# First cross-attention scores placed among the last transposes of the first norm, the last query projection in halves behind them

## Chip, cores and metric

The kernel runs on one core of one Trainium2 chip. The metric is the device time of one execution in microseconds (us); lower is better.

## The reference

A decoder layer with the norm behind each part, on x of 2 x 1024 tokens with 256 features (2048 tokens in all), in float32:

```
x = layernorm(x + causal_self_attention(x))          # 16 heads of 16
x = layernorm(x + cross_attention(x, ctx, mask))     # 64 context rows per batch, biases, 16 heads
x = layernorm(x + mixture_of_experts(x))             # 16 experts, 4 per token, one shared expert
```

What the change touches is the seam between the first two lines. Of the cross-attention:

```
q = split_heads(queries @ Wq + bq)
scores = einsum('bhqd,bhkd->bhqk', q, k) / sqrt(16)
scores = where(mask, -1e15, scores)
attn = softmax(scores); ctx = einsum('bhqk,bhkd->bhqd', attn, v)
```

## The kernel before

The work goes over 16 tiles of 128 tokens (NT = 16; tiles 0 to 7 are the first batch, TB = 8). Every engine has its own program, written out by hand, and takes it strictly in order; semaphores are the only link. The result of a matmul goes to one of eight banks of `ps`.

**First norm.** TensorE (the loop over `t` in `range(NT + 4)`, L1634) writes the output projection of tile t to bank t % 2 (L1641). VectorE adds it to x and takes the statistics (`norm_stats`, L1061 to L1067), GpSimd the reciprocal root (`power`, L758), VectorE applies both (`norm_apply`, L1072) and counts `ln_done`. TensorE, three tiles behind, transposes the normed tile (`transpose_x`, L1631) and ScalarE copies it to `xT` (L863, `xT_kept`). In the same loop ScalarE rounds expert weights (`w_high`, L856), GpSimd subtracts (`w_low`, L765), and VectorE keeps the keys and values of the context (`keep_kv`, L1046 and L1054; `kv_kept` is 20 at the end).

**Query projection.** Behind every fourth transposed tile TensorE projects the queries of these four tiles, 512 columns, in two halves of 128 features, o = 0 and 1, to banks 6 and 7 (L1657, four matmul records each; `xq_ready`). ScalarE copies each half with its bias to `q2` (L870, `xq_kept`). Halves 7 and 8 are those of tiles 12 to 15.

**Cross-attention.** It follows one list, `XO`, that each engine reads. Step n works on half o = n % 2 of the heads of tile n // 2. The kinds that matter here, with their lags in steps: "S" (lag 0), scores on TensorE to bank n % 2: two records of q times keys (L1729) and one of the mask (L1731); VectorE takes the maximum (L1310) and subtracts it (L1314, `xs_sub`), ScalarE the exponential (L889, `xp_exp`), and at odd n with n // 2 below 4 a pair of expert weights (L856). "T" (lag 2): TensorE transposes the exponentials (L1738), ScalarE copies them (L896, `xpT_kept`). "V" (lag 4): times the values (L1748). "P", "Y" (lags 5 and 6, at odd steps): transpose (L1758) and output projection (L1765), and with "Y" the second norm begins, its root on GpSimd (L758). "X", "L": transpose of the normed tile and the router's logits (L1783). GpSimd waits for `xq_ready` to be 8, clears `biased` (L772) and then at each "S" below 16 adds a bias to a tile of x (L777), with a pair of `w_low` at each odd one.

TensorE enters the list behind these waits: `ln_in` NT, `xT_kept` NT, `kv_kept` 20, `xq_kept` 8, `mask_ready` 1. `xq_kept` 8 means that the last half of the last projection is copied. Scores 0 and 1 need queries of tile 0 alone.

Behind the cross-attention come the routing, the scatter of the rows (L788), the shared expert, 79 blocks of expert work and the last norm.

Of the kernel before, what the change touches and what calls it, by code (L numbers as in the profile page):

```python
# [28 lines left out]
ACT = mybir.ActivationFunctionType  # L29
AX = mybir.AxisListType  # L30

P = 128
B, S, D, H, DH = 2, 1024, 256, 16, 16
KC = D // P
T = B * S
NT = T // P
TB = S // P
S2 = 64
# [24 lines left out]
CH = 512  # L63
# [127 lines left out]
def build(nc, a, out, qk_parts, l_dram, slots, sums_of, marks):  # L191
    with ExitStack() as ctx:
# [18 lines left out]
        xT = sb("x_T", [P, KC, T], F32)  # L211
# [17 lines left out]
        kbd = vg_flat[:, 0:2048].rearrange("p (o b h k) -> p o b h k", o=2, b=B, h=8)  # L229
# [15 lines left out]
        q2 = on_mem[:, 0:4096].rearrange("p (o t) -> p o t", o=2)  # L245
# [25 lines left out]
        mask = wqkv_mem[:, 3 * D:3 * D + NT * S2 // 2].bitcast(BF16).rearrange("p (t k) -> p t k", t=NT)  # L271
        w_mem = sb("w_o1_xqkv", [P, 2048], F32)
        wo1 = w_mem[:, 0:512].rearrange("p (c n) -> p c n", c=GB // 2)
        wxq, wxk, wxv = (w_mem[:, 512 * i:512 * i + 512].rearrange("p (c n) -> p c n", c=KC) for i in (1, 2, 3))
        used = [0]

        def over_w(words):
# [14 lines left out]
        bq = sb("b_q", [P, 2], F32)  # L292
# [3 lines left out]
        identb = sb("ident_b", [P, P], BF16)  # L296
# [61 lines left out]
               for u, at in enumerate((0, 512, 2048))]  # L358
        hsp = nc.alloc_sbuf_tensor_at("block_h", [P, 3, 2, P], F32R, offset=on_at + 4 * (4096 + 3072))
        ps = ctx.enter_context(nc.psum_tensor("ps", [P, 8, CH], F32))  # L360
# [22 lines left out]
        y_ready, ln_in, ln_chain, ln_pow, ln_done, xT_ready, xT_kept = (  # L383
            sem(n) for n in ("y_ready", "ln_in", "ln_chain", "ln_pow", "ln_done", "xT_ready", "xT_kept"))
        kv_ready, kv_kept, mask_ready, xq_ready, xq_kept = (
            sem(n) for n in ("kv_ready", "kv_kept", "mask_ready", "xq_ready", "xq_kept"))
        xs_ready, xs_max, xs_sub, xp_exp, xpT_ready, xpT_kept, xo_recip, xo_norm, xoT_ready = (
            sem(n) for n in ("xs_ready", "xs_max", "xs_sub", "xp_exp", "xpT_ready", "xpT_kept", "xo_recip", "xo_norm",
                             "xoT_ready"))
# [410 lines left out]
        def _(act):  # L800
            for n in range(NQK):
# [11 lines left out]
                if n >= 4:  # L813
                    t, more = n % 2, 1 + (n - 4) // 2
# [34 lines left out]
            act.wait_ge(ld_late, 16 * 16)  # L849
            act.wait_ge(b_ready, NB * NG)  # L850

            def w_high(e):

                act.wait_ge(ld_we[e // 4], 32)
                for raw, high in zip(raw_of(e), part_of(e, 0)):
                    nc.scalar.activation(high, raw, ACT.Copy).then_inc(w_hi, 1)  # L856

            for t in range(NT + 1):
                if W_TILE <= t < NT:
                    w_high(t - W_TILE)  # L860
                if t < NT:
                    act.wait_ge(xT_ready, t + 1)
                    nc.scalar.activation(xT[:, :, P * t:P * t + P],  # L863
                                         ps[:, 2 + t % 2, 0:D].rearrange("p (c s) -> p c s", c=KC),
                                         ACT.Copy).then_inc(xT_kept, 1)
                if t and t % 4 == 0:
                    for o in range(2):
                        n = (t // 4 - 1) * 2 + o
                        act.wait_ge(xq_ready, n + 1)
                        nc.scalar.activation(q2[:, o, CH * (t // 4 - 1):CH * (t // 4)], ps[:, 6 + o, :],  # L870
                                             ACT.Identity, bias=bq[:, o:o + 1]).then_inc(xq_kept, 1)
            def shared(c):
                act.wait_ge(g_ready, c + 1)
                wait(act, h_done, c - 1)
# [7 lines left out]
                                         ps[:, c % 2 + 2 * u, :], ACT.Copy).then_inc(y_moved, 1)  # L882

            for kind, n in XO:
                if kind == "S":
                    act.wait_ge(xs_sub, n + 1)
                    if n >= 2:
                        act.wait_ge(xpT_ready, n - 1)
                    nc.scalar.activation(px[:, n % 2, :], sx[:, n % 2, :], ACT.Exp, scale=SCALE).then_inc(xp_exp, 1)  # L889
                    if n % 2 and W_ACT + n // 2 < E:  # L890
                        w_high(W_ACT + n // 2)
                if kind == "T":
                    act.wait_ge(xpT_ready, n + 1)
                    if n >= 2:
                        act.wait_ge(xo_ready, n - 1)
                    nc.scalar.activation(pTx[:, n % 2].rearrange("p r s -> p (r s)"), ps[:, 2 + n % 2, :],  # L896
                                         ACT.Copy).then_inc(xpT_kept, 1)
                if kind == "O":
                    act.wait_ge(xoT_ready, n + 1)
                    if n >= 2:  # L900
                        act.wait_ge(y_ready, NT + n - 1)
                    nc.scalar.activation(oTx[:, n % 2].rearrange("p o s -> p (o s)"), ps[:, 5, 0:D],
                                         ACT.Copy).then_inc(xo_kept, 1)
                if kind == "Z":
                    act.wait_ge(ln_shift, n + 1)
                    nc.scalar.activation(x[:, n, :], x[:, n, :], ACT.Identity, bias=nmr[:, n % 4:n % 4 + 1],
                                         scale=rstd[:, n % 4:n % 4 + 1]).then_inc(ln_done, 1)
                if kind == "X":
                    act.wait_ge(xT_ready, NT + n + 1)
                    nc.scalar.activation(xT[:, :, P * n:P * n + P],  # L910
                                         ps[:, 7, 0:D].rearrange("p (c s) -> p c s", c=KC),
                                         ACT.Copy).then_inc(xT_kept, 1)
                if kind == "L":
                    act.wait_ge(r_logit, n + 1)
                    size = GROUPS[n]
                    nc.scalar.activation(score[:, FIRST[n]:FIRST[n + 1], :],
                                         ps[:, 7, D:D + size * E].rearrange("p (t e) -> p t e", t=size),
                                         ACT.Exp, scale=-1.0).then_inc(r_kept, 1)
                if kind == "E":
                    shared(n)  # L920
                if kind == "A" and n >= 2:
                    move_y(n)
# [578 lines left out]
        def _(pe):  # L1501
# [67 lines left out]
            for kind, n in P1:  # L1569
                if kind in ("qk0", "qk1"):  # L1570
                    b, o, t = QK[n]
# [57 lines left out]
            def transpose_x(t, bank):  # L1629
                for k in range(KC):  # L1630
                    last = nc.tensor.transpose(ps[:, bank, P * k:P * k + P], x[:, t, P * k:P * k + P], identf[:])  # L1631
                last.then_inc(xT_ready, 1)

            for t in range(NT + 4):  # L1634
                if t < NT:
                    if t >= 2:
                        pe.wait_ge(ln_in, t - 1)
                    pe.wait_ge(o_done, (t // TB + 1) * GB // 2)
                    for q in range(GB // 2):
                        pair = on[:, t // TB * GB + 2 * q + 1, P * (t % TB):P * (t % TB) + P]  # L1640
                        last = nc.tensor.matmul(ps[:, t % 2, 0:D], pair, wo1[:, q, :], start=(q == 0),  # L1641
                                                stop=(q == GB // 2 - 1))
                    last.then_inc(y_ready, 1)
                s = t - 3
                if 0 <= s < NT:
                    pe.wait_ge(ln_done, s + 1)
                    if s >= 2:
                        pe.wait_ge(xT_kept, s - 1)
                    transpose_x(s, 2 + s % 2)
                s -= 1  # L1650
                if s >= 0 and s % 4 == 3:
                    pe.wait_ge(xT_kept, s + 1)
                    for o in range(2):
                        if s >= 4:
                            pe.wait_ge(xq_kept, s // 4 * 2 + o - 1)
                        for k in range(KC):
                            last = nc.tensor.matmul(ps[:, 6 + o, :], wxq[:, k, P * o:P * o + P],  # L1657
                                                    xT[:, k, P * (s - 3):P * (s + 1)], start=(k == 0), stop=(k == KC - 1))
                        last.then_inc(xq_ready, 1)

            def project(c, part):

# [52 lines left out]
                last.then_inc(r_rank, 1)  # L1715


            pe.wait_ge(ln_in, NT)
            pe.wait_ge(xT_kept, NT)
            pe.wait_ge(kv_kept, 20)  # L1720
            pe.wait_ge(xq_kept, 8)
            pe.wait_ge(mask_ready, 1)
            tiles, logits = 0, 0
            for kind, n in XO:
                if kind == "S":
                    t, o = n // 2, n % 2
                    if n >= 2:
                        pe.wait_ge(xs_sub, n - 1)
                    nc.tensor.matmul(ps[:, n % 2, :], q2[:, o, P * t:P * t + P],  # L1729
                                     kbd[:, o, t // TB].rearrange("p h k -> p (h k)"), start=True, stop=False)  # L1730
                    nc.tensor.matmul(ps[:, n % 2, :], identb[:], mask[:, t, :].unsqueeze(1).to_broadcast([P, 8, S2]),  # L1731
                                     start=False, stop=True).then_inc(xs_ready, 1)
                if kind == "T":
                    pe.wait_ge(xp_exp, n + 1)
                    if n >= 2:
# [5 lines left out]
                if kind == "V":  # L1741
                    t, o = n // 2, n % 2
# [218 lines left out]
```

## Time and profile before

| | |
|---|---|
| median of 3 runs | 642.4 us (641.43 to 643.92) |
| profiled execution, its own time | 642.46 us |
| its span, first to last instruction | 640.7 us |
| mean granted TensorE clock | 0.977 |
| busy: TensorE, VectorE, ScalarE, GpSimd | 91%, 74%, 57%, 48% |
| first scores of the cross-attention start at | 340.9 us |

The span is from the first to the last instruction; the time of an execution is a little longer. A granted clock of 1.00 is the full one (2.4 GHz), 0.50 the lower one (1.2 GHz).

### The profile page before, as it was taken

To read this page: it belongs to the slowest core of one execution; us is meant where nothing else is said; L and a number is where in the kernel's file an instruction comes from. 1 tells how busy PE (TensorE), PEld (TensorE's weight loads), DVE (VectorE), ACT (ScalarE), POOL (GpSimd) and SP (SyncE) were. 2 spreads that over 40 slices of the span, in tenths; PEclk is the share of its full clock that TensorE was granted. 3 is DMA by queue.
4 is the path that set the end of the run, shared out by engine and by line. 5 is a ranking of instruction groups with operands and counts; after the bars stand their busy time and mean duration, and the time that the engine had idled before them with its cause. 6 is when DMAs were issued, how large, how long until landed. Compare 5 with 4: busy or idle time off the path is not lost.

```text
span 640.7 us, 12791 instructions
## 1 busy us (share of the span) xinstructions
PE 583.5 (91%) x3766; PEld 356.6 (56%) x3766; DVE 475.0 (74%) x1306; ACT 364.1 (57%) x742; POOL 310.2 (48%) x395
## 2 busy tenths in 40 slices
PE   6978899999999999898879999999877999998994
PEld 2634434433343443225444777778546899998861
DVE  2388788887888889305965787776555987998896
ACT  2335366766666676782464644535315677776645
POOL 5414314142533433255587550647564777775650
PEclk9999899999999999999999998979987999999999
DMA  5967797172543710002930000212234896669957
GB/s 183 204 179 160 137 276 104 26 104 56 71 86 53 109 25 3 20 20 71 381 127 0 1 2 1 79 64 85 86 107 135 247 293 224 213 190 305 318 181 249
DMA packets 47773, 82.92 MB, mean 129 GB/s; under 512 B 12023, under 2 KB 28919, under 8 KB 45815
## 3 DMA queue, kind: packets, MB, share of 16 engines
q1 hardware_dynamic: 40844, 62.68, 39.0%
q0 software_dynamic: 6864, 19.44, 8.2%
q8 instruction: 33, 0.54, 0.4%
q14 instruction: 32, 0.25, 0.1%
HBM read 53.81 MB, written 32.48 MB: 135 GB/s over the span
## 4 chain that ended last, share of the span: by engine, by line
PE 53%; DVE 23%; DMA 8%; issue 5%; SPq 4%; ACT 4%; POOL 3%; POOLq 0%; DVEq 0%; ACTq 0%
DVE neg_max L986 9%; PE ps L1540 8%; PE ps L1564 8%; PE ps L1831 6%; PE ps L1521 4%; PE ps L1729 3%; PE ps L1854 3%; PE ps L1748 3%; DMA v_group<-expert_slots 3%; DMA stacks<-m_rows 2%; PE ps L1810 2%; POOL expert_slots L788 2%; PE ps L1765 2%; PE ps L1578 2%; ACT temps L831 2%
## 5 line engine op out<-in xcount | busy, mean ns | idle before, releaser
L986 DVE TENSOR_REDUCE neg_max<-ps 128x1 f32<-128x512 f32 (+3 forms) x304 | 181.5, 654 | 29.9 <-PE ps L1526 15.9
L831 ACT ACTIVATE temps<-ps 128x1024 f32<-128x1024 f32 (+1 forms) x192 | 146.4, 812 | 72.3 <-PE ps L1540 72.0
L724 POOL TENSOR_SCALAR_AFFINE_SELECT temps<-temps 128x256 f32<-128x256 f32 x128 | 52.3, 412 | 141.7 <-ACT temps L831 140.3
L1540 PE MATMUL ps<-stacks 99*128 99x512 bf16 (+3 forms) x384 | 94.3, 331 | 4.5 <-DMA stacks<-m_rows 2.9
L795 POOL DMA_INDIRECT expert_outputs<-x_T,w_o_xqkv x79 | 78.1, 988 | 32.8 <-issue 16.8
L1521 PE MATMUL ps<-stacks 96*128 96x512 bf16 (+3 forms) x320 | 86.9, 320 | 7.1 <-DVE neg_max L986 6.8
L1564 PE MATMUL ps<-temps,v_group 128*32 128x512 f32 (+3 forms) x768 | 81.8, 498 | 1.7 <-POOL temps L724 0.6
L788 POOL DMA_INDIRECT expert_slots<-x_tok,w_o_xqkv x64 | 62.5, 976 | 26.5 <-issue 17.2
L1831 PE MATMUL ps<-w_split,block_x 128*128 x474 | 71.9, 289 | 0.7 <-DVE block_x L1398 0.7
L1540 PEld LDWEIGHTS ps<-stacks 99*128 99x128 bf16 x384 | 27.2, 98 | 75.2 <-ACT temps L831 55.5
L1831 PEld LDWEIGHTS ps<-w_split,block_x 128*128 128x128 f32 x474 | 63.8, 195 | 1.1 <-issue 1.1
L1521 PEld LDWEIGHTS ps<-stacks 96*128 96x128 bf16 x320 | 30.9, 98 | 38.3 <-DVE neg_max L986 21.1
L1854 PE MATMUL ps<-w_split,block_h 128*128 x237 | 48.6, 314 | 0.3 <-ACT x_T L951 0.3
L758 POOL TENSOR_TENSOR ln_rstd<-ln_var_eps,minus_half 128x1 f32<-128x1 f32 x32 | 18.8, 589 | 60.4 <-DVE ln_var_eps L1067 60.3
L889 ACT ACTIVATE o_norm<-o_norm 128x512 f32<-128x512 f32 x32 | 20.1, 629 | 48.5 <-DVE o_norm L1314 48.4
L1526 PE MATMUL ps<-stacks 128*128 128x128 bf16 x256 | 44.4, 221 | 2.9 <-DVE neg_max L986 1.6
L938 ACT ACTIVATE o_norm<-ps 128x128 f32<-128x128 f32 x79 | 21.9, 278 | 31.2 <-PE ps L1831 30.2
L1578 PE MATMUL ps<-x_T,w_qkv 128*128 128x512 f32 x64 | 31.9, 639 | 6.0 <-DMA x_T<-in_xT 6.0
L1398 DVE TENSOR_TENSOR block_x<-ps,block_x 128x256 fp32r<-128x256 f32 x79 | 33.1, 420 | 5.5 <-ACT block_x L930 4.3
L1729 PE MATMUL ps<-v_group,o_norm 128*128 128x512 f32 x64 | 34.8, 627 | 1.4 <-ACT o_norm L870 1.0
L1310 DVE TENSOR_REDUCE x_max<-ps 128x8 f32<-128x512 f32 x32 | 22.1, 690 | 18.3 <-PE ps L1731 17.8
L704 POOL TENSOR_TENSOR temps<-temps 128x1024 bf16<-128x1024 f32 (+1 forms) x10 | 17.4, 1741 | 36.9 <-ACT temps L812 36.9
(221 smaller groups left out, 1085.2 us busy)
## 6 DMA issues: line engine op xcount, KB each, us to landing
stacks<-qk_parts SPq DMA_DIRECT2D x96, 128.0 KB
v_group<-expert_slots SPq DMA_DIRECT2D x79, 138.5 KB
qk_parts<-temps SPq DMA_DIRECT2D x6, 768.0 KB, 4.6
w_raw<-in_w SPq DMA_DIRECT2D x4, 1024.0 KB, 10.1
early_parts<-expert_outputs SPq DMA_DIRECT2D x4, 1024.0 KB, 8.1
expert_slots<-in_pad SPq DMA_DIRECT2D x16, 138.5 KB
expert_slots<-in_pad SPq DMA_DIRECT2D x1, 2077.5 KB
x_T<-in_xT SPq DMA_DIRECT2D x4, 512.0 KB, 6.3
```

Source lines behind the costliest of these rows:

```text
L724: nc.gpsimd.affine_select(diag, diag, [[0, 2], [1, P]], ALU.is_ge, zero, base=0, channel_multiplier=-1).then_inc(b_cut, 1)
L788: pool.indirect_dma_start(slots, bass.IndirectOffsetOnAxis(ridx[:, t, k:k + 1].bitcast(U32), 0), xe[:, t, :], None).then_inc(scattered[q], 16)
L795: pool.indirect_dma_start(sums_of, bass.IndirectOffsetOnAxis(idxs[:, b:b + 1].bitcast(U32), 0), yb[:, b % YB, :], None).then_inc(landed[b ...
L831: nc.scalar.activation(pt[:, n % 4, :, 0:w], ps[:, 2 + 2 * (n % 2):4 + 2 * (n % 2), 0:w], ACT.Exp, scale=SCALE).then_inc(b_exp, 1)
L986: nc.vector.tensor_reduce(nmx[:, c, h0:h0 + nh, i], ps[:, A_BANKS[n % 3], 0:w * nh].rearrange("p (h k) -> p h k", h=nh), axis=AX.X, op=ALU ...
L1521: last = nc.tensor.matmul(ps[:, A_BANKS[n % 3], w * s:w * s + plain], qs[0:KR, ua, h0 + s, P * i:P * i + P], ks[0:KR, ua, h0 + s, CH * c:C ...
L1540: last = nc.tensor.matmul(ps[:, bank, 0:w], ks[0:KM, u, 2 * pr + s, P * j:P * j + P], qs[0:KM, u, 2 * pr + s, q0:q0 + w], start=True, stop ...
L1564: last = nc.tensor.matmul(ps[HS * h:HS * h + HS, 6, CH - w:CH], vg[:, u, j, h, :], pt[:, (2 * p + h // 2) % 4, h % 2, 0:w], start=(j == 0) ...
L1578: last = nc.tensor.matmul(ps[:, 2 + 2 * (n % 2) + q, :], wqkv[:, t, k, P * o:P * o + P], xT[:, k, S * b + CH * q:S * b + CH * q + CH], sta ...
L1729: nc.tensor.matmul(ps[:, n % 2, :], q2[:, o, P * t:P * t + P], kbd[:, o, t // TB].rearrange("p h k -> p (h k)"), start=True, stop=False)
L1831: last = nc.tensor.matmul(ps[:, 2 + b % 2, 0:D], xsp[b % 3][:, xp, k, :], w13s[:, bass.ds(expert[b], 1), wp, at:at + 2 * INTER], start=(k ...
L1854: last = nc.tensor.matmul(ps[:, 6 + b % 2, 0:D], hsp[:, b % 3, hp, :], w2s[:, bass.ds(expert[b], 1), wp, :], start=(n == 0), stop=(n == 2))
```

## The change

Scores 0 and 1 leave the head of the list on TensorE and stand in the loop of the first norm, ahead of the wait for the norm of tile 15 and its transposes. They wait for `kv_kept` 20, `mask_ready` 1, `xq_kept` 6 (three of the four query projections) and `ln_in` 15 and 16 (their banks). The last query projection leaves the loop: its half o = 0 stands ahead of scores 2, its half o = 1 ahead of scores 3, and ScalarE's two copies of the halves stand ahead of exponentials 2 and 3. The list is entered behind `xT_kept` NT alone; `xq_kept` 8 is waited for ahead of scores 24 (tile 12), the first that need it. VectorE's and GpSimd's programs are as before.

```diff
@@ ScalarE
+            def keep_queries(c, o):
+
+                act.wait_ge(xq_ready, 2 * c + o + 1)
+                nc.scalar.activation(q2[:, o, CH * c:CH * c + CH], ps[:, 6 + o, :],
+                                     ACT.Identity, bias=bq[:, o:o + 1]).then_inc(xq_kept, 1)
...
-                if t and t % 4 == 0:
+                if t and t % 4 == 0 and t < NT:
                     for o in range(2):
-                        n = (t // 4 - 1) * 2 + o
-                        act.wait_ge(xq_ready, n + 1)
-                        nc.scalar.activation(q2[:, o, CH * (t // 4 - 1):CH * (t // 4)], ps[:, 6 + o, :],
-                                             ACT.Identity, bias=bq[:, o:o + 1]).then_inc(xq_kept, 1)
+                        keep_queries(t // 4 - 1, o)
...
             for kind, n in XO:
+                if kind == "S" and n in (2, 3):
+                    keep_queries(NT // 4 - 1, n - 2)
@@ TensorE
+            def query_projection(c, o):
+
+                pe.wait_ge(xT_kept, 4 * c + 4)
+                if c:
+                    pe.wait_ge(xq_kept, 2 * c + o - 1)
+                for k in range(KC):
+                    last = nc.tensor.matmul(ps[:, 6 + o, :], wxq[:, k, P * o:P * o + P],
+                                            xT[:, k, CH * c:CH * c + CH], start=(k == 0), stop=(k == KC - 1))
+                last.then_inc(xq_ready, 1)
+
+            def cross_scores(n):
+
+                t, o = n // 2, n % 2
+                nc.tensor.matmul(ps[:, n % 2, :], q2[:, o, P * t:P * t + P],
+                                 kbd[:, o, t // TB].rearrange("p h k -> p (h k)"), start=True, stop=False)
+                nc.tensor.matmul(ps[:, n % 2, :], identb[:], mask[:, t, :].unsqueeze(1).to_broadcast([P, 8, S2]),
+                                 start=False, stop=True).then_inc(xs_ready, 1)
+
+            def early_scores():
+
+                pe.wait_ge(kv_kept, 20)
+                pe.wait_ge(mask_ready, 1)
+                pe.wait_ge(xq_kept, 6)
+                for n in range(2):
+                    pe.wait_ge(ln_in, NT - 1 + n)
+                    cross_scores(n)
...
                 s = t - 3
                 if 0 <= s < NT:
+                    if s == NT - 1:
+                        early_scores()
                     pe.wait_ge(ln_done, s + 1)
...
                 s -= 1
-                if s >= 0 and s % 4 == 3:
-                    pe.wait_ge(xT_kept, s + 1)
+                if 0 <= s < NT - 1 and s % 4 == 3:
                     for o in range(2):
-                        if s >= 4:
-                            pe.wait_ge(xq_kept, s // 4 * 2 + o - 1)
...
+                        query_projection(s // 4, o)
...
-            pe.wait_ge(ln_in, NT)
             pe.wait_ge(xT_kept, NT)
-            pe.wait_ge(kv_kept, 20)
-            pe.wait_ge(xq_kept, 8)
-            pe.wait_ge(mask_ready, 1)
...
+                if kind == "S" and n in (2, 3):
+                    query_projection(NT // 4 - 1, n - 2)
+                if kind == "S" and n >= 2:
+                    if n == NT + TB:
+                        pe.wait_ge(xq_kept, 8)
+                    pe.wait_ge(xs_sub, n - 1)
+                    cross_scores(n)
```

## Rows read from the trace of the kernel before

**Rows 1.** The page: TensorE's busy time, and the granted clock by fortieths of the span.
```profile
PE 583.5 (91%) x3766; PEld 356.6 (56%) x3766; DVE 475.0 (74%) x1306; ACT 364.1 (57%) x742; POOL 310.2 (48%) x395
...
PEclk9999899999999999999999998979987999999999
```

**Rows 2.** Chain that ended last, 330 to 352: start us, us, what.
```profile
330.53 0.69 ACT o_norm L870
...
334.56 5.41 PE ps L1657 x8
...
339.99 0.70 ACT o_norm L870
...
340.93 1.10 PE ps L1729 x2
...
342.28 0.70 DVE x_max L1310
...
343.75 1.12 PE ps L1729 x2
344.88 0.22 PE ps L1731
345.09 0.44 PE ps L1738 x4
...
347.04 0.86 PE ps L1729 x2
```

**Rows 3.** Timeline of TensorE: start us, us, instructions, [idle before, its releaser].
```profile
324.14 0.44 PE L1631 MATMUL ps<-ident_f,x_tok 128*128 128x128 f32 x2 [0.39 <-DVE x_tok L1072]
...
326.89 3.60 PE L1657 MATMUL ps<-x_T,w_o_xqkv 128*128 128x512 f32 x8
...
333.36 0.44 PE L1631 MATMUL ps<-ident_f,x_tok 128*128 128x128 f32 x2 [2.03 <-DVE x_tok L1072]
...
342.94 0.38 PE L1731 MATMUL ps<-w_qkv,ident_b 128*128 128x512 bf16 x1
```

**Rows 4.** Timeline of VectorE.
```profile
331.96 1.35 DVE L1072 TENSOR_SCALAR x_tok<-x_tok,ln_mean_var,ln_rstd 128x256 f32<-128x256 f32 x1 [1.13 <-POOL ln_rstd L758]
342.28 0.69 DVE L1310 TENSOR_REDUCE x_max<-ps 128x8 f32<-128x512 f32 x1 [8.97 <-PE ps L1731]
343.01 0.69 DVE L1314 TENSOR_TENSOR o_norm<-ps,x_max 128x512 f32<-128x512 f32 x1
```

**Rows 5.** Timeline of GpSimd.
```profile
340.02 0.37 POOL L772 MEMSET w_o_xqkv<- 128x320 f32 x1 [6.13 <-PE ps L1657]
...
351.21 1.97 POOL L765 TENSOR_TENSOR w_split<-w_raw,w_split 128x512 fp32r<-128x512 f32 x2
359.11 0.55 POOL L758 TENSOR_TENSOR ln_rstd<-ln_var_eps,minus_half 128x1 f32<-128x1 f32 x1 [5.94 <-DVE ln_var_eps L1067]
```

**Rows 6.** Windows: stretch, us, busy by engine (instructions), granted clock, DMA share, GB/s.
```profile
386.00:390.00 4.00, 4.00 (x17) 2.83 (x16) 2.35 (x5) 0.85 (x3) 0.00 (x0) 0.57 0.00 0
...
442.00:446.00 4.00, 4.00 (x38) 3.90 (x37) 1.54 (x5) 2.03 (x5) 3.06 (x5) 1.00 0.28 106
```

**Rows 7.** Windows around the last query projection; busy: TensorE, weight loads, VectorE, ScalarE, GpSimd.
```profile
331.40:334.50 3.10, 0.44 (x2) 0.20 (x2) 1.35 (x1) 3.10 (x9) 2.49 (x4) 1.00 0.00 0
335.30:338.80 3.50, 3.50 (x5) 1.35 (x4) 0.00 (x0) 0.69 (x1) 0.00 (x0) 0.51 0.00 0
```

**Rows 8.** Timeline of ScalarE.
```profile
324.61 0.38 ACT L863 ACTIVATE x_T<-ps 128x256 f32<-128x256 f32 x1 [0.31 <-PE ps L1631]
...
328.81 0.69 ACT L870 ACTIVATE o_norm<-ps,b_q 128x512 f32<-128x512 f32 x1 [1.34 <-PE ps L1657]
...
334.12 0.38 ACT L863 ACTIVATE x_T<-ps 128x256 f32<-128x256 f32 x1
...
343.73 0.63 ACT L889 ACTIVATE o_norm<-o_norm 128x512 f32<-128x512 f32 x1 [3.05 <-DVE o_norm L1314]
...
345.59 0.92 ACT L856 ACTIVATE w_split<-w_raw 128x512 fp32r<-128x512 f32 x2
```

More of the change, by code:

```diff
@@ L1650, in _ @@
                 s -= 1
-                if s >= 0 and s % 4 == 3:
-                    pe.wait_ge(xT_kept, s + 1)
+                if 0 <= s < NT - 1 and s % 4 == 3:
                     for o in range(2):
-                        if s >= 4:
-                            pe.wait_ge(xq_kept, s // 4 * 2 + o - 1)
[L1656 to L1659, printed above, removed]
+                        query_projection(s // 4, o)
             def project(c, part):
@@ L1715, in ranks @@
                 last.then_inc(r_rank, 1)
-            pe.wait_ge(ln_in, NT)
             pe.wait_ge(xT_kept, NT)
-            pe.wait_ge(kv_kept, 20)
-            pe.wait_ge(xq_kept, 8)
-            pe.wait_ge(mask_ready, 1)
             tiles, logits = 0, 0
             for kind, n in XO:
[L1725 to L1732, printed above, removed]
+                if kind == "S" and n in (2, 3):
[5 more added lines that the diff above has]
+                    cross_scores(n)
                 if kind == "T":
```

## The prediction

> **What bounds the kernel now.** I read the page first: TensorE is busy 91% of the span [rows 1]. That share is a mean over stages, so I went to the place of the change, between 326 and 352 us. The view to read there is the chain of waits, which names at every moment the work that the end hung on [rows 2]. The reader sees one thread with no alternative: ScalarE keeps the sixth half of the queries (330.53) and goes on with expert weights and tile copies; then come eight matmuls of the last query projection (334.56, 5.41 us), ScalarE's copy of its second half (0.70), the first scores on TensorE, VectorE's maximum (0.70) and subtraction (0.70), and from 343.75 on TensorE without a gap: scores, transposes, scores. The engines one by one say who was idle meanwhile. TensorE waited 2.03 us ahead of the transposes of tile 15, for VectorE [rows 3]. VectorE ended the norm of tile 15 at 333.31 and had nothing until 342.28, 8.97 us [rows 4]. GpSimd had nothing for 6.13 us up to 340.02, when the last half of the projection was done [rows 5]. So up to 343.75 the stage is a relay with latency in it, and behind that it is bound by TensorE; the windows further on show TensorE busy 4.00 of 4.00 us [rows 6], so what the relay loses, the end loses, and what it saves, the end gets, if the later stages are only shifted.
>
> Last I looked at the granted clock. It is 1.00 while TensorE has 0.44 us of work in the 3.10 us from 331.4, and 0.51 in the 3.50 us from 335.3, though the engine is then busy all the time [rows 7]: it ran at 1.2 instead of 2.4 GHz behind the gap. Eight matmuls of the same shape took 3.60 us at 326.89 [rows 3].
>
> **The change, part by part.** Nothing is removed from the work: the eight records of the last projection, its two query copies and the six records of scores 0 and 1 have other places.
>
> *Scores 0 and 1 ahead of the transposes of tile 15.* They wait for the sixth query copy, which ends at 330.53 + 0.69 = 331.22 [rows 2]; for the banks of the output projections of tiles 14 and 15, for the keys and for the mask, all of which VectorE has done before its norm at 331.96 and the 1.13 us of idle time ahead of it [rows 4], as it takes its queue in order. From the end of a query copy to the first score goes 0.24 us (339.99 + 0.70 to 340.93) [rows 2], so scores 0 begin at 331.46. Today the pair runs from 340.93 until the next instruction could start 0.22 us into the second mask matmul, at 342.94 + 0.22 = 343.16 [rows 2, 3]: 2.23 us. The pair ends so at 333.69, in the gap of 2.03 us. The transposes that stand behind it start at 333.69 instead of 333.36: 0.33 us late. What is late next is ScalarE's copy of tile 15. It starts 0.47 us behind its transposes where ScalarE is free (324.14 to 324.61) [rows 3, 8], so at 334.16; today it starts at 334.12, since ScalarE was with weights until then (busy 3.10 of the 3.10 us from 331.4) [rows 7, 8]. The edit therefore costs 0.04 us of the 0.33, and the projection starts at 334.60. Without that cover of ScalarE it would cost all 0.33.
>
> *VectorE.* Scores 0 are ready 1.35 us behind their start (340.93 to 342.28), at 332.81, so VectorE goes straight on at 333.33: maximum, subtraction, maximum, subtraction, at 0.70 each (342.28 to 343.01 is 0.73 from start to start) [rows 2, 4]; it ends the second subtraction at 336.2. ScalarE starts its exponential 0.72 us behind the start of a subtraction (343.01 to 343.73) [rows 2, 8]: 334.8 and 336.2. All of this now lies beside the projection.
>
> *The halves of the last projection.* Four matmuls are 3.60 / 2 = 1.8 us, or 1.73 in the chain's counting, where eight stand with 3.45 once the pipe is filled. TensorE's queue is then: half 0 (334.60 to 336.33), scores 2 (0.86 + 0.22 = 1.08, to 337.41), transposes 0 (0.44, to 337.85), half 1 (1.73, to 339.58), scores 3 (to 340.66), transposes 1 (to 341.10), scores 4. One start behind a wait costs 0.26 us more (1.12 + 0.22 at 343.75 against 1.08) [rows 2], so scores 4 start at 341.36, against 347.04 now. Each wait in it is met. Exponential 0 is there at 335.4 for transposes 0. Scores 4 want subtraction 2, which ends near 339.3. Transposes 2 want exponential 2 (near 339.9; ahead of it is the first query copy, which is ready at 334.60 + 1.92 = 336.5, the 1.92 being from the start of a half to its copy, 326.89 to 328.81 [rows 3, 8], but stands behind expert 12's weights of 0.92 us until 337.6). The tightest is ScalarE's second probability copy: in its queue stand between 336.7 and 344.5 two weight pairs (0.92 each), two query copies (0.69), exponentials 2 and 3 (0.63) and copies 0 and 1 [rows 8], and exponential 3 waits for VectorE until 342.5; it ends near 344.5, and TensorE wants it for transposes 3 near 344.7. That is a margin of 0.2 us, and I put 0.2 us in the sum for it. If the cover is gone, each us by which ScalarE is late is a us lost.
>
> *What else is queued behind the moved steps.* On ScalarE the query copies stand ahead of exponentials 2 and 3. On GpSimd the memset waits for the eighth half: 337.85 + 1.92 + about 0.2 = 340.0, and today it starts at 340.02; so GpSimd keeps its old times while the others come forward. Its queue of eight additions of the bias and four weight pairs runs to 351.21 + 1.97 = 353.18, and the first reciprocal root of the second norm is wanted at 359.11 [rows 5], which comes forward to 353.4. Slack 5.94 us before, 0.2 after, and VectorE takes the root only behind another maximum and subtraction. From there a pair of tiles costs GpSimd less than TensorE, and the slack grows again. I cost it at nothing. The edits move no DMA and pass no wait of SP; SP's next wait in this stage is for the last scores. The wait for the eighth copy, now ahead of scores 24, is met some 15 steps earlier.
>
> **The sum.** 347.04 - 341.36 = 5.68 us earlier. It splits in two: the projection took 5.41 where 3.45 would do (1.96 us, the clock), and 3.7 us are the last query copy, the first scores' latency and VectorE's pair, now beside other work. With the 0.2 of margin, 5.5. From the profiled execution, 642.46 us (span 640.7, and 1.8 around it): 642.46 - 5.5 = **637.0 us**. The median of the runs shown is 642.40, so the same sum holds against it.
>
> *Bounds.* What the trace can't show is the clock in the new order. At worst the two halves run as now: 1.96 us are not won, gain 3.5. If they ran wholly at the lower clock the eight would take 6.9 us and the gain would be 5.5 - 3.45 = 2.1. At best ScalarE's margin holds and the gain is 5.7. I take the full clock, since the gap of 3.10 us with 0.44 us of work gets 2.23 us of scores, and the gaps left are of about 0.5 us, of which the run at the full clock ahead has such ones too (0.39 us at 324.14) [rows 3]. Further on there are stretches at the lower clock while TensorE is busy without a gap: in the 4 us from 386 the granted clock is 0.57, which costs 4.00 x (1.00 - 0.57) = 1.7 us; from 442, in a stretch with the same steps of the third group of tiles, it is 1.00 [rows 6]. So such a stretch can come or stay away when the work is shifted, plus or minus 1.7 us for each.
>
> The Trainium skill, TensorE: Matmul & The Clock Gate, section Part 1: The HAM clock gate, says that the monitor runs on its own time, not the kernel's, so that the same kernel changes clock at other places from run to run. By it the 1.96 us need not be in every run of the kernel before, and the median would win between 3.5 and 5.5 us. The trace neither agrees nor disagrees, being of one execution; that the stretches at 386 and 442 differ speaks for it [rows 6].
>
> **The rivals.**
> (a) *The clock part is not won*, because the clock still falls in the new order, or because most runs of before don't have the fall there. For it: 386 and 442 differ [rows 6]. Against it: the profiled execution stands at the median. Gain 3.5: **638.9 us**. The Trainium skill, TensorE: Matmul & The Clock Gate, section Part 1: The HAM clock gate, would let one expect this one.
> (b) *ScalarE becomes the bound in the first eight steps.* For it: a margin of 0.2 us by my own count. Against it: it was idle in the relay (3.05 us ahead of the first exponential alone) [rows 8], and what it gains there it can spend. If its two weight pairs and two query copies are paid in full (2 x 0.92 + 2 x 0.69 = 3.2), the gain is 5.7 - 3.2 = 2.5: **640.0 us**, within 0.5%.
> (c) *The scores are not early*: some wait ahead of them (the sixth copy, the keys) holds them and with them tile 15. Then only the order of the halves changes; one half (1.73) leaves the path to scores 0 but is paid behind it: gain 0, **642.5 us**. Against it: the sixth copy ends at 331.22, and VectorE was through with all that the scores want at 331.96 - 1.13 = 330.83 [rows 2, 4].
> (d) *Slower*: behind the new start the lower clock lasts longer in the part that TensorE bounds (now 343.75 to 386, at 1.00). A us at half the clock loses half a us, so it decides from 2 x 5.5 = 11.0 us of it on; 18 us of it lose 9.0: **646.0 us**. Nothing in the profile speaks for it but that the fall at 386 came while the engine was busy; against it, no fortieth of the span (16 us) has a clock below seven tenths, so none holds more than 0.6 x 16 = 9.6 us at the lower one [rows 1].
>
> **How the numbers follow.** The forecast 0.60, (a) 0.22, (b) 0.10, (c) 0.05, (d) 0.03. The forecast's own range is 635.3 to 638.7, one stretch of 1.7 us either way. The range for 8 in 10 must take in (a): 635.0 to 640.0; (b), (c) and (d) are left out. A change of 0.5% is 3.2 us, about what a measurement of this kernel can tell from none. Faster by more than that, below 639.2: the forecast and most of (a), 0.79. Within: the rest of (a), (b), (c), 0.18. Slower: 0.03.
>
> **What the changed profile would show.** Scores 0 and 1 start at 331.5, and the transposes of tile 15 near 333.7; VectorE's gap of 8.97 us is gone; the projection shows as two groups of four at near 334.6 and 337.9 with 592 ns a matmul and a granted clock of 1.00; scores 4 start near 341.4; GpSimd's memset stays at 340.0 and the first root shows no wait for it. I am wrong if the halves run at a clock of 0.5, if TensorE is idle for ScalarE between 341 and 346, if the first root starts more than 0.6 us behind its input, or if the later stages come forward by less than 5 us.

## The result and the profile after

The changed kernel took 636.28 us in the median of four runs (632.51 to 642.1), the kernel before 643.07 us (641.43 to 643.92). The ratio is 0.9881, with a 95% interval of 0.9833 to 0.993: faster by 7.6 us, or by 4.5 to 10.7. In a second comparison, with 12 runs of the changed kernel (experiment e4), the ratio was 0.9931 (0.9894 to 0.9968), 4.4 us. The two intervals share 0.9894 to 0.993, which is 4.5 to 6.8 us; the first rests on three executions of the changed kernel, the second on twelve.

The execution whose trace is shown here took 642.1 us; the comparison leaves it out as disturbed, as it leaves out one execution of experiment e3, of 3110.05 us, and five of the 33 of before that stand beside e1 to e4. Its stages can be read against those of before, its span can't. First the page, as in [rows 1]: the busy shares are the same, and the slices with a low clock lie elsewhere.

```profile
span 640.4 us, 12795 instructions
...
PE 584.1 (91%) x3766; PEld 357.3 (56%) x3766; DVE 474.6 (74%) x1306; ACT 363.5 (57%) x742; POOL 309.6 (48%) x395
...
PEclk9999799999999999989999999879987999999999
```

Now the timeline of TensorE in the changed kernel, which answers to [rows 3]. L1636 are the transposes, L1652 and L1654 the scores, L1645 the projection, L1761 the transposes of the exponentials.

```profile
333.94 0.44 PE L1636 MATMUL ps<-ident_f,x_tok 128*128 128x128 f32 x2 [0.17 <-DVE x_tok L1077]
334.52 1.10 PE L1652 MATMUL ps<-v_group,o_norm 128*128 128x512 f32 x2
...
336.53 0.38 PE L1654 MATMUL ps<-w_qkv,ident_b 128*128 128x512 bf16 x1
336.75 0.38 PE L1636 MATMUL ps<-ident_f,x_tok 128*128 128x128 f32 x2
337.66 1.96 PE L1645 MATMUL ps<-x_T,w_o_xqkv 128*128 128x512 f32 x4 [0.53 <-ACT x_T L869]
339.45 1.02 PE L1652 MATMUL ps<-v_group,o_norm 128*128 128x512 f32 x2
```

Everything here is 3.05 us later than in the trace of before (tile 14's transposes at 333.94 instead of 330.89), though no code ahead of it was changed. That offset comes from two stretches at the lower clock, one longer near 74 us and one near 273 us that before didn't have. I therefore measure from the transposes of tile 14, the last thing common to both, and not from the start of the span.

The scores of tile 0 start 0.58 us behind them and fill the gap in which TensorE waited 2.03 us; the transposes of tile 15 start at +2.81 instead of +2.47, and the projection at +3.72 instead of +3.67. The chain of waits, as in [rows 2], then goes through TensorE alone.

```profile
337.66 1.96 PE ps L1645 x4
339.61 0.86 PE ps L1652 x2
340.47 0.22 PE ps L1654
340.69 0.44 PE ps L1761 x4
341.12 1.72 PE ps L1645 x4
342.84 0.86 PE ps L1652 x2
343.70 0.22 PE ps L1654
343.92 0.44 PE ps L1761 x4
344.36 0.86 PE ps L1652 x2
```

Scores 4 start 344.36 - 333.94 = 10.42 us behind the transposes of tile 14, against 347.04 - 330.89 = 16.15 before: 5.73 us. At the first router logits (381.71 and 384.39 in TensorE's timeline) it is 47.77 against 53.50, again 5.73: TensorE bounds what lies between, and nothing is given back there. Behind it something is: at the second router logits, those of the next group of tiles, the lead is 4.16 us in this pair of traces (79.75 against 83.91), and the part on the time comes back to it. VectorE and GpSimd, as in [rows 4] and [rows 5]: VectorE's wait of 8.97 us ahead of the first maximum is gone, GpSimd's memset stands 8.97 us behind tile 14's transposes instead of 9.13, and the root of the second norm waits 0.37 us for its input instead of 5.94.

```profile
335.01 1.36 DVE L1077 TENSOR_SCALAR x_tok<-x_tok,ln_mean_var,ln_rstd 128x256 f32<-128x256 f32 x1 [1.13 <-POOL ln_rstd L758]
...
336.29 0.68 DVE L1315 TENSOR_REDUCE x_max<-ps 128x8 f32<-128x512 f32 x1
```

```profile
342.91 0.37 POOL L772 MEMSET w_o_xqkv<- 128x320 f32 x1 [5.96 <-PE ps L1645]
...
356.43 0.55 POOL L758 TENSOR_TENSOR ln_rstd<-ln_var_eps,minus_half 128x1 f32<-128x1 f32 x1 [0.37 <-DVE ln_var_eps L1072]
```

Last the windows, as in [rows 6] and [rows 7] (busy: TensorE, weight loads, VectorE, ScalarE, GpSimd; then clock, DMA). The clock stays at 1.00 at the seam. At 386, where before had 0.57, it is 1.00, and it is low from 398, where before it was not.

```profile
335.30:338.80 3.50, 2.97 (x10) 1.44 (x9) 3.43 (x5) 2.89 (x8) 1.65 (x2) 1.00 0.00 0
386.00:390.00 4.00, 4.00 (x25) 2.97 (x25) 3.73 (x21) 1.39 (x3) 0.55 (x1) 1.00 0.00 0
398.00:402.00 4.00, 4.00 (x17) 3.14 (x18) 2.56 (x5) 2.50 (x5) 3.12 (x3) 0.62 0.19 71
```

### The profile page after: what moved, and what is told of

It reads as the page before. It is cut to its first block, busy times and chain, and to the rows that moved or that the text cites. A ratio compares the mean times of both kernels' runs of the same rounds, so it can differ in the third digit from the quotient of the medians.

```text
span 640.4 us, 12795 instructions
## 1 busy us (share of the span) xinstructions
PE 584.1 (91%) x3766; PEld 357.3 (56%) x3766; DVE 474.6 (74%) x1306; ACT 363.5 (57%) x742; POOL 309.6 (48%) x395
## 4 chain that ended last, share of the span: by engine, by line
PE 48%; DVE 23%; DMA 9%; issue 6%; POOL 5%; ACT 4%; SPq 4%; POOLq 0%; DVEq 0%; ACTq 0%
DVE neg_max L991 8%; PE ps L1545 8%; PE ps L1569 8%; PE ps L1526 5%; PE ps L1854 4%; DMA v_group<-expert_slots 3%; PE ps L1652 3%; PE ps L1771 3%; POOL expert_outputs L795 2%; DMA stacks<-m_rows 2%; PE ps L1788 2%; POOL expert_slots L788 2%; ACT temps L831 2%; PE ps L1877 2%; PE ps L1761 2%
## 5 line engine op out<-in xcount | busy, mean ns | idle before, releaser
L1652 PE MATMUL ps<-v_group,o_norm 128*128 128x512 f32 x64 | 35.1, 631 | 0.1
L1877 PEld LDWEIGHTS ps<-w_split,block_h 128*128 128x128 f32 x237 | 33.6, 189 | 2.4 <-issue 0.5
```

The source lines that it names most:

```text
L1877: last = nc.tensor.matmul(ps[:, 6 + b % 2, 0:D], hsp[:, b % 3, hp, :], w2s[:, bass.ds(expert[b], 1), wp, :], start=(n == 0), stop=(n == 2))
```

## The experiments

All stages below are measured in TensorE's timeline from the transposes of tile 14. "S4" is the start of scores 4, "logits" that of the first router logits. All times are us. "logits 2" is the start of the router logits of the next group, and "against before" is taken at the first. The chain of waits puts the start of scores 4 some 0.16 us later than the timeline (16.15 and 10.42 instead of 15.99 and 10.25); the expectations of e1 to e4 use the chain's numbers.

| kernel | S4 | logits | logits 2 | against before | ratio of times (95%) |
|---|---|---|---|---|---|
| before | 15.99 | 53.50 | 83.91 | | |
| changed | 10.25 | 47.77 | 79.75 | -5.73 | 0.9881 (0.9833 to 0.993) |
| e4, changed again | 10.26 | 47.77 | 79.76 | -5.73 | 0.9931 (0.9894 to 0.9968) |
| e1, early scores only | 10.70 | 48.21 | 80.21 | -5.29 | 0.990 (0.9862 to 0.9937) |
| e2, halves only | 11.37 | 48.89 | 79.22 | -4.61 | 0.9942 (0.9908 to 0.9977) |
| e3, before with the gap filled | 14.34 | 51.86 | 83.85 | -1.64 | 0.998 (0.9947 to 1.0014) |
| f2, more work on ScalarE | 10.24 | 48.57 | 80.56 | | one run |
| f3, more work on GpSimd | 10.25 | 49.91 | 78.67 | | one run |
| f1, g1, g2: before again | 15.76, 15.75, 15.99 | 53.28, 53.27, 53.51 | 82.04, 82.03, 82.27 | | one run each |

The medians of the whole times are 637.86 us (e1), 639.52 (e2), 643.17 (e3), 639.4 (e4) and 643.94 (before). They don't rank the parts: e1 stands below the whole change.

**e1: the early scores alone.** The projection is whole again.

```diff
@@ TensorE, against the changed kernel
             pe.wait_ge(xT_kept, NT)
+            for o in range(2):
+                query_projection(NT // 4 - 1, o)
...
-                if kind == "S" and n in (2, 3):
-                    query_projection(NT // 4 - 1, n - 2)
@@ ScalarE
-                if t and t % 4 == 0 and t < NT:
+                if t and t % 4 == 0:
...
-                if kind == "S" and n in (2, 3):
-                    keep_queries(NT // 4 - 1, n - 2)
```

> One part of the change alone: scores 0 and 1 early, the last projection whole again between the transposes of tile 15 and scores 2, both query copies ahead of exponential 0. I measure the stage from the start of the transposes of tile 14 to the start of scores 4; it is 347.04 - 330.89 = 16.15 us before and 344.36 - 333.94 = 10.42 us in the changed kernel. My theory (TensorE's queue sets the end, and its sum is the same in either order): 10.4 us, and the time of the changed kernel within 0.3%. Rival (cutting the projection is what wins, since exponential 0 is late behind a whole one): exponential 0 ends some 1 to 2 us later, TensorE waits for it ahead of transposes 0, and the stage is 11.4 to 12.2 us.

The stage is 10.70, 0.45 above the changed kernel (10.25, which is the 10.4 of my theory in the chain's counting): neither that nor the rival's 11.4 to 12.2, but the rival's mechanism at a smaller size. ScalarE's queue and TensorE's show it:

```profile
341.93 0.69 ACT L855 ACTIVATE o_norm<-ps,b_q 128x512 f32<-128x512 f32 x1 [1.03 <-PE ps L1643]
342.52 1.14 ACT L892 ACTIVATE o_norm<-o_norm 128x512 f32<-128x512 f32 x2
```

```profile
341.73 1.02 PE L1650 MATMUL ps<-v_group,o_norm 128*128 128x512 f32 x2
342.59 0.38 PE L1652 MATMUL ps<-w_qkv,ident_b 128*128 128x512 bf16 x1
343.19 0.66 PE L1759 MATMUL ps<-ident_f,o_norm 128*128 128x128 f32 x4 [0.22 <-ACT o_norm L892]
```

Exponential 0 stands behind both query copies, which wait for the whole projection, and TensorE waits for it ahead of transposes 0. This part of the change alone gives 5.29 of the 5.73 us, the clock's part included (it is at 1.00 at the seam here too), and the halves add 0.44 (48.21 - 47.77). The whole times don't resolve 0.44 us.

**e2: the halves alone.** Scores 0 and 1 stand behind the transposes of tile 15.

```diff
@@ TensorE, against the changed kernel
-                    if s == NT - 1:
-                        early_scores()
...
+            early_scores()
             pe.wait_ge(xT_kept, NT)
```

> The other part alone: the projection in halves ahead of scores 2 and 3, but scores 0 and 1 behind the transposes of tile 15, while TensorE waits for ScalarE's copy of that tile. The stage from the transposes of tile 14 to scores 4: my theory says that scores 0 and 1 (2.23 us) fill the 0.8 us wait and cost the rest, so 10.4 + 1.4 - 0.1 = 11.7 us at the full clock, 4.4 us less than before. Rival (the clock still falls, as TensorE has its gap of 2.0 us ahead of tile 15): up to 1.7 us more, 13.4 us. Time about 637.5 to 639.

11.37 (I had 11.7, from the chain's counting; in the timeline's that is 11.5), and the clock stays at 1.00 in this one trace, so the rival falls. The time of 639.52 us lies above the 637.5 to 639 I gave. Here the gap of 2.04 us ahead of tile 15 is open, but TensorE works from there on:

```profile
332.70 0.44 PE L1636 MATMUL ps<-ident_f,x_tok 128*128 128x128 f32 x2 [2.04 <-DVE x_tok L1077]
332.98 1.04 PE L1652 MATMUL ps<-v_group,o_norm 128*128 128x512 f32 x2
333.85 0.38 PE L1654 MATMUL ps<-w_qkv,ident_b 128*128 128x512 bf16 x1
334.07 1.02 PE L1652 MATMUL ps<-v_group,o_norm 128*128 128x512 f32 x2
334.93 0.38 PE L1654 MATMUL ps<-w_qkv,ident_b 128*128 128x512 bf16 x1
335.14 1.88 PE L1645 MATMUL ps<-x_T,w_o_xqkv 128*128 128x512 f32 x4
```

The place of the early scores, ahead of tile 15 or behind it, is worth 1.12 us. The 4.61 that e2 wins without it have two sources: scores 0 and 1 don't stand behind the projection and its last copy, and the clock doesn't fall, which e3 prices at 1.65 us. e2 is therefore not the halves by themselves, since it moves scores 0 and 1 ahead of the projection as well.

**e3: the clock by itself.** The kernel before, with the scores of tile 0 issued once more in the gap, unread.

```diff
@@ TensorE, against the kernel before
                 if 0 <= s < NT:
+                    if s == NT - 1:
+                        pe.wait_ge(kv_kept, 20)
+                        pe.wait_ge(mask_ready, 1)
+                        pe.wait_ge(xq_kept, 6)
+                        for o in range(2):
+                            pe.wait_ge(ln_in, NT - 1 + o)
+                            nc.tensor.matmul(ps[:, o, :], q2[:, o, 0:P], kbd[:, o, 0].rearrange("p h k -> p (h k)"),
+                                             start=True, stop=False)
+                            nc.tensor.matmul(ps[:, o, :], identb[:],
+                                             mask[:, 0, :].unsqueeze(1).to_broadcast([P, 8, S2]),
+                                             start=False, stop=True)
                     pe.wait_ge(ln_done, s + 1)
```

> The kernel before, with the six matmul records of scores 0 and 1 issued a second time ahead of the transposes of tile 15, where the changed kernel has them; nobody reads these, and all else is as before. It measures the clock's part by itself. My theory: the last projection takes 3.5 us instead of 5.4, the granted clock stays 1.00, and the stage from the transposes of tile 14 to scores 4 is 16.15 - 1.96 = 14.2 us. Rival (the lower clock has nothing to do with the gap): 16.2 us. The time falls by 0 to 2 us, as not every run of before need have the fall.

The eight records take 3.70 us instead of 5.40, and the stage is 14.34, 1.65 less. More work in the gap makes the kernel faster there: the lower clock was the gap's. Its size is 1.65 to 1.70 us; I had compared the projection at the lower clock with one that starts without a wait (3.45). The relay behind it is as before:

```profile
333.87 0.38 PE L1631 MATMUL ps<-ident_f,x_tok 128*128 128x128 f32 x2
334.74 3.70 PE L1668 MATMUL ps<-x_T,w_o_xqkv 128*128 128x512 f32 x8 [0.49 <-ACT x_T L863]
339.45 1.10 PE L1740 MATMUL ps<-v_group,o_norm 128*128 128x512 f32 x2 [1.01 <-ACT o_norm L870]
```

It also shows the price of the filling: the transposes of tile 15 start at +2.81 instead of +2.47, and the projection at +3.68 instead of +3.67. ScalarE covers it. In the whole time 1.6 us is not resolved (0.998), and in this trace it is gone at the second logits (83.85 against 83.91), after a stretch at the lower clock near 398 us.

**e4: the changed kernel again.**

> The changed kernel itself, for a second profile and more runs beside the parts. The stage from the transposes of tile 14 to scores 4 is 10.4 us again, within 0.1; what lies outside it (the stretches at the lower clock) may be elsewhere. Time 636 us, 5 to 8 less than before. If the win were luck of the clock, the stage would differ from 10.4 by more than 1 us.

10.26 to scores 4 and 47.77 to the logits, as the first time. The time was 639.4 us beside 643.94 for before, in the median: 4.5 us, just under the 5 to 8 I gave, and 3.4 us above the 636 us.

**f1, g1, g2: is the fall of the clock in every execution of before?** No edit.

> The kernel before, for a second profile of its own. Theory of the prediction's rival (a): the fall of the clock at the last projection is not in every execution. If it is there again, the projection takes 5.2 to 5.5 us and the stage from the transposes of tile 14 to scores 4 (first records in TensorE's timeline) 16.0 us; if not, 3.7 and 14.3 us, and the change is worth 4.1 us in such a run instead of 5.7.

> The kernel before once more, to see how often the clock falls at its last projection; two profiles of two show it. Theory (it comes at every execution, since the gap of 3.1 us with 0.44 us of work is in each): stage from the transposes of tile 14 to scores 4 of 15.8 to 16.0 us. Rival (by chance): 14.3 us in this one or the next.

> As the run before it: 15.8 to 16.0 us with the fall, 14.3 us without.

It is there in all three, so in four of four: 15.75 to 15.99. Against f1 and g1 the change is worth 5.5 us at the logits, and e3's filling 1.4. The timeline of g2:

```profile
334.44 0.44 PE L1631 MATMUL ps<-ident_f,x_tok 128*128 128x128 f32 x2 [2.03 <-DVE x_tok L1072]
335.64 5.40 PE L1657 MATMUL ps<-x_T,w_o_xqkv 128*128 128x512 f32 x8 [0.76 <-ACT x_T L863]
```

The falls further on do come and go. The windows of g2 have 1.00 at 386 and 418 (in [rows 6] 386 is at 0.57, and 442 at 1.00), and f1 has one at 446:

```profile
386.00:390.00 4.00, 4.00 (x29) 3.33 (x30) 2.14 (x5) 1.62 (x5) 0.00 (x0) 1.00 0.00 0
398.00:402.00 4.00, 2.60 (x17) 1.84 (x16) 3.73 (x16) 1.39 (x3) 0.64 (x2) 1.00 0.00 0
418.00:422.00 4.00, 4.00 (x28) 3.20 (x28) 3.73 (x21) 1.39 (x3) 3.02 (x4) 1.00 0.28 106
```

```profile
446.00:450.00 4.00, 3.91 (x18) 3.08 (x17) 2.98 (x12) 1.58 (x4) 2.96 (x4) 0.57 0.25 94
```

**f2: ScalarE's margin.** Expert 13's weights are copied twice behind exponential 3.

```diff
@@ ScalarE, against the changed kernel
+            act.wait_ge(ld_we[3], 32)
             for kind, n in XO:
...
+                    if n == 3:
+                        for raw, high in zip(raw_of(W_ACT + 1), part_of(W_ACT + 1, 0)):
+                            nc.scalar.activation(high, raw, ACT.Copy).then_inc(again, 1)
+                        act.wait_ge(again, 2)
                     if n % 2 and W_ACT + n // 2 < E:
                         w_high(W_ACT + n // 2)
```

> The changed kernel with expert 13's two weight copies on ScalarE done twice behind exponential 3 (0.92 us more in its queue). It measures ScalarE's margin, which the prediction gave as 0.2 us. From the transposes of tile 14 to scores 6 is 348.92 - 333.94 = 14.98 us in the changed kernel. Theory: probability copy 1 was done 0.3 us before transposes 3 wanted it, and beyond that each us is lost, so 15.6 us. Rival (TensorE's queue has room there): 15.0 us.

The start of scores 6 is at 15.79 instead of 14.98: 0.81 lost. The margin is read one step ahead of it, at the place that the prediction names. ScalarE's second probability copy starts 0.96 us later (13.79 instead of 12.83), and transposes 3, which wait for it, 0.77 us later (14.51 instead of 13.74): the margin was 0.2 us. TensorE waits 0.62 us ahead of transposes 3, where it doesn't in the changed kernel. The copy in the changed kernel, the copy in f2 and the transposes in f2:

```profile
346.77 0.57 ACT L901 ACTIVATE o_norm<-ps 128x512 f32<-128x512 f32 x1
...
344.91 0.58 ACT L907 ACTIVATE o_norm<-ps 128x512 f32<-128x512 f32 x1
```

```profile
345.63 0.63 PE L1767 MATMUL ps<-ident_f,o_norm 128*128 128x128 f32 x4 [0.62 <-ACT o_norm L907]
```

**f3: GpSimd's margin.** Its memset is done six times.

```diff
@@ GpSimd, against the changed kernel
             pool.wait_ge(xq_ready, 8)
+            for i in range(5):
+                nc.gpsimd.memset(biased, -3e38).then_inc(again, 1)
+                pool.wait_ge(again, i + 1)
             nc.gpsimd.memset(biased, -3e38).then_inc(filled, 1)
```

> The changed kernel with GpSimd's memset done six times instead of once, about 2.1 us more ahead of its additions and weight pairs. It measures GpSimd's margin. The first root of the second norm then starts about 1.8 us late. Theory (the root is wanted by VectorE only behind a maximum and a subtraction, and VectorE is idle 0.97 us behind that): from the transposes of tile 14 to the first logits it stays 381.71 - 333.94 = 47.8 us, at most 48.0. Rival (the slack of 0.4 us is all there is): 49.4 us.

The logits come at 49.91, 2.14 us late, and both theories fall: my 48.0 at most, and the rival's 49.4, which counted the delay beyond the slack. GpSimd had 2.1 us more to do and 0.37 us of slack, so the root started 1.70 us late (24.19 instead of 22.49), and 2.14 us were lost. The timelines of GpSimd, VectorE, ScalarE and TensorE show how:

```profile
357.52 0.57 POOL L759 TENSOR_TENSOR ln_rstd<-ln_var_eps,minus_half 128x1 f32<-128x1 f32 x1
358.04 1.43 POOL L781 TENSOR_TENSOR x_tok<-x_tok,w_qkv 128x256 f32<-128x256 f32 x2
...
359.40 1.97 POOL L766 TENSOR_TENSOR w_split<-w_raw,w_split 128x512 fp32r<-128x512 f32 x2
```

```profile
358.13 3.26 DVE L1119 SCALAR_TENSOR_TENSOR ln_minus_mean<-ln_mean_var,ln_rstd 128x1 f32<-128x1 f32 x1 [1.07 <-POOL ln_rstd L759]
```

```profile
361.42 0.60 ACT L915 ACTIVATE x_tok<-x_tok,ln_minus_mean,ln_rstd 128x256 f32<-128x256 f32 x1 [2.94 <-DVE ln_minus_mean L1119]
```

```profile
362.07 0.44 PE L1640 MATMUL ps<-ident_f,x_tok 128*128 128x128 f32 x2 [1.82 <-ACT x_tok L915]
```

VectorE's product of one column, which takes 0.15 us in its median, took 3.26 us. It began 0.09 us behind the start of GpSimd's bias additions, and ended at 361.39 as GpSimd's weight pair ended at 361.37. In the changed kernel the root is done before VectorE wants it, and the product is issued at 357.59, where it takes 0.15 us, though GpSimd is at its bias additions then too (356.94 to 358.35; the first of them ends 0.09 us later). The loss hangs on this one long product. Had it taken 0.7 us, TensorE's input would have been there near 359.5 (an estimate: 358.13 + 0.7, and the 0.68 us that went here from the product's end to the transposes), and TensorE was busy until 360.25: my theory would have held.

## Why the prediction was right

**The relay.** In the stage it held nearly to the digit. The sum put scores 4 5.68 us earlier, and the traces have 5.73, at scores 4 and at the first logits, and again in e4. The start of the projection was predicted 0.04 us late beside 0.33 us of later transposes; measured 0.05 beside 0.34 (and 0.01 in e3). The queue of halves, scores and transposes took the predicted 1.08 and 0.44; the halves took 1.96 and 1.72.

**The split of the sum.** The clock is worth 1.65 us, not 1.96 (e3; 1.4 against f1 and g1), and the overlap 4.1 us, not 3.7. The error is in the term, not in the sum: the price of a start behind a wait (0.26 us) belonged to the projection on both sides, and I had charged it to the new order alone and left it out of the 3.45.

**What each part is worth.** The prediction gave the halves no price of their own. e1 and e2 show that either part takes most of the gain: 5.29 for the early scores, 4.61 for the halves with the scores moved no further than ahead of the projection. They overlap, since each takes scores 0 and 1 out from behind the projection and its copy, and each keeps the clock at 1.00 at the seam.

**The margins.** I put 0.2 us in the sum for ScalarE's; nothing was lost, and the margin is 0.2 us by f2. GpSimd's slack was given as 0.2 us and is 0.37; the first root was to show no wait and shows these 0.37. But the cover that I named behind it, that VectorE takes the root only behind a maximum and a subtraction, doesn't hold as I meant it: f3 shows that once the root is late, the product that follows can meet GpSimd's next instructions, and in that trace the loss was larger than the lateness beyond the slack.

The Trainium skill, SBUF — State Buffer, section Who interferes with whom, says that a VectorE instruction with two inputs in SBUF and a GpSimd instruction that reads SBUF can't run at once, and that the second waits until the first is done. By that rule f3's product, with its two inputs of one column, waits; the trace agrees, with 3.26 us for 0.15. It lasted over four GpSimd instructions, though, not only over the first; three later products of the same run, issued 0.05 to 0.15 us behind the start of an addition, took 0.51 to 0.69 us and ended with that one. Why this one did not is open.

**Rival (a), the clock part not won.** It fell: the fall is in four of four profiles of before, in none of the changed kernel's two, and in none of e1, e2, e3, f2 and f3. The rule of the Trainium skill, TensorE: Matmul & The Clock Gate, section Part 1: The HAM clock gate, that the places of the changes vary from run to run, is borne out by the stretches from 386 on, and not by the one at the seam, which came each time at most 0.3 us apart in what it cost (53.27 to 53.51 to the logits).

**Rivals (b), (c) and (d).** ScalarE did not become the bound, and the scores were early (0.58 us behind tile 14's transposes); either rival would show in the 47.77. (d) did not come as written, since TensorE was at 1.00 all the way to the logits. But its mechanism, a lower clock behind the new start while TensorE is busy, came further on: from the first to the second logits the changed kernel took 31.98 us, and e4 31.99, where f1, g1, g2 and f3 took 28.76.

```profile
394.00:398.00 4.00, 2.74 (x13) 1.76 (x14) 3.31 (x14) 1.26 (x4) 1.77 (x3) 0.88 0.00 0
398.00:402.00 4.00, 4.00 (x16) 3.57 (x15) 2.07 (x4) 2.62 (x6) 1.90 (x2) 0.50 0.29 106
402.00:406.00 4.00, 4.00 (x22) 2.83 (x21) 2.49 (x7) 0.38 (x1) 1.60 (x2) 0.77 0.00 0
```

These are windows of e4. The fall comes behind a gap of 1.14 us at 396.31, in which TensorE waits for VectorE; all eleven traces have that gap (at 403.61 in f1), and five of them, before, f1, g1, g2 and f3, have no fall behind it. The stretch costs 3.2 us there, so at the second logits the lead over before is 4.2 us (its trace has 1.65 us of its own fall at 386 in it) and over f1, g1 and g2 2.3 to 2.5. That is one of the signs that the prediction named for being wrong: later stages forward by less than 5 us. The step behind it is the premise that the later stages are only shifted; the bounds had allowed 1.7 us either way for each such stretch.

**The time.** 637.0 was forecast and 636.28 measured. That they lie so close is in part luck. The change wins 5.7 us up to the first logits, or 5.5 against f1 and g1; what of it reaches the end the whole times alone tell, with 7.6 us in the first comparison and 4.4 (2.1 to 6.8) in e4's. e4's median of 639.4 us lies outside the forecast's own range of 635.3 to 638.7, nearer to rival (a)'s 638.9, though not by rival (a)'s mechanism. From the first logits to the end took 256.3 us in the trace of before, 253.5, 253.7 and 253.8 in f1, g1 and g2, but 258.7 in the changed kernel and 258.2 in e4, for the same work; much of that goes with the falls of the clock, which lie at 386 in one and at 398 in another. Whether the change makes the fall near 398 likelier is open: both profiles of the changed kernel have it, and e1, e2, e3 and f2, but f3 doesn't, and none of the four of before does. e3, which has it too, keeps the old order, so the early scores as such are not its cause; what the six with it have in common is that the clock did not fall at the seam, which holds for f3 as well.

## What to carry to other kernels

At the seam of two stages, look for work of the next stage that needs only what is done long since, and put it where the bounding engine waits for the last piece of the stage before; here 2.2 us of scores cost 0.05 us and, with the projection in halves behind them, took 4 us of latency off the relay. Ask of the engine that waits not only how long it idles but what clock it has behind the gap: filling the gap with unread work alone gave back 1.65 us in the stage, though nothing that the whole time resolved. Follow the gain to the next stages, too: of the 5.73 us at the first logits 4.16 were left at the second in the same pair of traces. And when a stage comes forward, recount the slack of the engines that don't: GpSimd's fell from 5.94 to 0.37 us, and 2.1 us more work there cost 2.14 in the one trace taken.

## What the runs showed of the hardware

A VectorE instruction of one element per partition, with two inputs in SBUF, took 3.26 us instead of 0.15 in f3, when it was issued 0.09 us behind the start of a row of four GpSimd instructions that work on SBUF, and it ended with the last of that row. That length was seen once. In every trace three more of these products, issued 0.05 to 0.15 us behind the start of an addition on GpSimd, took 0.50 to 0.69 us and ended with the one addition. The application of the norm shows the same kind of wait: 0.40 to 0.41 us for tiles 0 to 7, where no weight pair of GpSimd runs, 0.67 to 0.74 for tiles 8 to 14 and 1.35 to 1.36 for tile 15, each of these ending some 0.15 us behind a GpSimd weight subtraction that it began in.

Two gaps of TensorE of the same 2.0 us ahead of tile 15 had different ends. In the kernel before, followed by another 0.76 us gap, they led to the lower clock in four of four profiles; in e2, followed by work, they did not in the one that was taken.
